# A recurrent row with its causal mask added on TensorE, and the convolution of B and C summed there from four sets of weights

## The reference

```python
def mamba2(X, W_in, conv_w, conv_b, dt_bias, A_log, D, norm_w, W_out):
    z, xBC, dt = split(X @ W_in.T)                 # 256, 384, 4 features
    dt  = softplus(dt + dt_bias)
    xBC = silu(causal_conv(xBC, conv_w) + conv_b)  # 4 taps, each of 384 channels by itself
    x, B, C = split(xBC)                           # 256 (4 heads of 64), 64, 64
    # per head: h = h * exp(dt * A) + dt * B x ;  y = C . h
    y = scan(...) + D * x
    y = y * silu(z)
    y = y * rsqrt(mean(y * y) + 1e-5) * norm_w
    return y @ W_out.T
x = layernorm(x + (mamba2(x) + x))                 # eps 1e-5
x = layernorm(x + attention_and_experts(x))        # 16 heads, 8 experts, top 2
```

## Time and profile before

| | us |
|---|---|
| runs of the kernel before: median of 3, lowest to highest | 923.86 (921.42 to 941.75) |
| profiled execution: its own time / span of the core | 919.96 / 918.3 |
| busy: TensorE | 736.6 (80%) |
| VectorE | 638.8 (70%) |
| ScalarE | 474.1 (52%) |
| GpSimd | 437.8 (48%) |
| mean granted TensorE clock | 0.914 |

### The profile page before, as it was taken

One profiled execution on the slowest core, in us unless ns is written; L12 is line 12 of the kernel. 1 busy time (PEld: TensorE's weight loads), 2 busy tenths in 40 slices (PEclk: granted clock), 3 DMA queues, 4 the chain that ended last, 5 costly groups with the idle time before them and its releaser, 6 DMA issues. The chain is left out here.

```text
span 918.3 us, 18413 instructions
## 1 busy us (share of the span) xinstructions
PE 736.6 (80%) x5462; PEld 491.5 (54%) x5462; DVE 638.8 (70%) x1576; ACT 474.1 (52%) x983; POOL 437.8 (48%) x546
## 2 busy tenths in 40 slices
PE   5978888878853979898989998989788898999500
PEld 2656555655542534444444444444347897999500
DVE  4688988898752958596868496968524576557753
ACT  3555555665420036565656455656554465666524
POOL 1344455445632112236363436363514768767863
PEclk9999999999975559999999799999979999999955
DMA  2001223432113002225252523220151222325441
GB/s 55 18 19 29 86 81 125 143 118 70 29 58 124 21 23 66 79 73 152 75 148 79 117 74 107 74 69 25 38 173 51 76 63 81 90 62 152 124 117 46
DMA packets 97998, 73.66 MB, mean 80 GB/s; under 512 B 15559, under 2 KB 89651, under 8 KB 97902
## 3 DMA queue, kind: packets, MB, share of 16 engines
q1 hardware_dynamic: 93294, 63.89, 24.6%
q0 software_dynamic: 4608, 8.60, 2.7%
HBM read 42.39 MB, written 25.25 MB: 74 GB/s over the span
## 5 line engine op out<-in xcount | busy, mean ns | idle before, releaser
L1639 ACT ACTIVATE pb<-psB 128x512 f32<-128x512 f32 (+1 forms) x352 | 192.1, 559 | 199.2 <-PE psB L2075 175.4
L1744 DVE TENSOR_REDUCE mx<-psB 128x1 f32<-128x384 f32 (+3 forms) x352 | 207.3, 634 | 64.9 <-PE psB L2055 64.6
L2053 PE MATMUL psB<-kx,qx 72*128 72x384 bf16 (+3 forms) x512 | 144.6, 333 | 17.6 <-POOL hide L1499 14.9
L2075 PE MATMUL psB<-qx,kx 75*128 75x256 bf16 (+3 forms) x512 | 131.7, 313 | 20.0 <-DMA qx<-mparts 15.5
L1596 POOL TENSOR_SCALAR_AFFINE_SELECT pb<-pb 128x512 f32<-128x512 f32 x112 | 71.0, 639 | 159.4 <-ACT pb L1639 158.5
L2055 PE MATMUL psB<-hide,ident 128*128 128x128 bf16 x512 | 109.0, 238 | 0.0
L2094 PE MATMUL psB<-pb,vx 128*32 128x512 f32 (+3 forms) x1024 | 99.4, 463 | 0.5 <-POOL pb L1596 0.5
L1565 POOL DMA_INDIRECT results<-y_e,hin x78 | 78.3, 1004 | 39.4 <-ACT y_e L1678 20.0
L2164 PE MATMUL psB<-hT_e,w1t 128*128 128x128 f32 x624 | 84.4, 278 | 14.6 <-issue 7.7
L2075 PEld LDWEIGHTS psB<-qx,kx 75*128 75x128 bf16 x512 | 46.2, 101 | 91.9 <-ACT pb L1639 55.4
L2164 PEld LDWEIGHTS psB<-hT_e,w1t 128*128 128x128 f32 x624 | 76.3, 193 | 17.4 <-issue 15.4
(11 more groups left out here) (232 smaller groups left out, 1345.0 us busy)
## 6 DMA issues: line engine op xcount, KB each, us to landing
qx<-q_parts SPq DMA_DIRECT2D x96, 96.0 KB
kx<-k_parts SPq DMA_DIRECT2D x96, 96.0 KB
hin<-slots SPq DMA_DIRECT2D x78, 65.0 KB
ys<-results SPq DMA_DIRECT2D x16, 256.0 KB, 3.9
q_parts<-part SPq DMA_DIRECT2D x8, 384.0 KB
k_parts<-part SPq DMA_DIRECT2D x8, 384.0 KB
xin<-in_L_attn_X SPq DMA_DIRECT2D x8, 256.0 KB, 3.4
x_rows<-x1o SPq DMA_DIRECT2D x8, 256.0 KB, 2.3
```

Source lines behind the costliest of these rows:

```text
L1639: nc.scalar.activation(pb[step % PBUF][:, h0:h0 + heads, 0:width], src, ACT.Exp).then_inc(exp_ready, 2 if u == NEXP - 1 else 1)
L1744: nc.vector.tensor_reduce(mx[:, h0:h0 + heads, qt], ps[:, S_BANK + u % banks, 0:heads * width].rearrange("p (h n) -> p h n", n=width), AX. ...
L2053: nc.tensor.matmul(out, qx[q][0:QK_ROWS, h0 + j, qt * P:(qt + 1) * P], kx[q][0:QK_ROWS, h0 + j, 0:width], start=True, stop=False)
L2075: ins = nc.tensor.matmul(out, kx[q][0:MAX_ROWS, 4 * g + h0 + j, kt * P:(kt + 1) * P], qx[q][0:MAX_ROWS, 4 * g + h0 + j, kt * P:SEQ], start ...
```

## The change

- **Mask.** `seg` gets a second product that adds `cover` to its bank: 0 where the causal mask keeps and -3e38 where it does not, in bf16 through a bf16 identity, so that the exponential gives 0 there. `gm` goes; each `mm` reads G straight from PSUM, bank 3. The third state product, which writes bank 3, now waits for the fourth `mm`.
- **Convolution of B and C.** At the start the block's weights are scaled by each of the four taps (`wtap`), turned on TensorE and copied (`wtapT`). `conv_bc` then sums four products of shifted inputs in bank 6, and SiLU reads that bank with the bias. The block's taps on VectorE and ScalarE are gone. The taps of x stay.
- **Residual.** `x2` goes: `woutT` is halved, the residual adds `xin` itself, and the layer norm's eps is divided by 4. `xin` gets a third buffer, which the residual of its row frees.
- **Order within a row.** On TensorE `turn_x` and `turn_xc` move to the end of a row (the first for two rows ahead, into bank 2), `project_dt` up behind `sums`. On GpSimd the second `ra_step` of a row moves behind `rms`. On ScalarE the squares of b-1 stand around the `yT` copy, half before and half behind; SiLU of B and C comes ahead of that of x.
- **End of the stage.** On VectorE the last residual moves ahead of the `rest` steps of row 6, on GpSimd `norm` and `shift` of the last row move ahead, and on SyncE the stores of row 6 move ahead of the last bf16 copy.

The core of the diff:

```diff
         def seg(pe, row, c):
             pe.wait_ge(ra_ready, row(4, c + 1))
             if c >= 2:
                 pe.wait_ge(decay_ready, row(4, c - 1))
             nc.tensor.matmul(bank(4 + c % 2), after[:, :], ra[c % 2][:, :, :].rearrange("p h n -> p (h n)"),
-                             start=True, stop=True).then_inc(seg_ps, 1)
+                             start=True, stop=False)
+            nc.tensor.matmul(bank(4 + c % 2).rearrange("p (h n) -> p h n", n=P), ident16[:, :],
+                             cover[:, :].unsqueeze(1).broadcast_to([P, MH, P]), start=False, stop=True).then_inc(seg_ps, 1)
...
+                if load:
+
+                    ahead = it * 2 + p + 2
+                    if ahead >= XBUF:
+                        sp.wait_ge(r_ready, ahead - XBUF + 1)
+                    sp.dma_start(xin[ahead % XBUF][:, :, :], x_rows[ahead]).then_inc(x_in[ahead % XBUF], 16)
...
+            store_qkv(BATCH - 2)
             store_x1b(BATCH - 1)
-            store_qkv(BATCH - 2)
...
+            nc.gpsimd.affine_select(out=ident16[:, :], in_=ones[:, :], compare_op=ALU.is_equal, fill=0.0, base=0,
+                                    pattern=[[-1, P]], channel_multiplier=1).then_inc(consts, 1)
+            nc.gpsimd.memset(cover[:, :], -3e38).then_inc(consts, 1)
+            pool.wait_ge(consts, 10)
+            nc.gpsimd.affine_select(out=cover[:, :], in_=cover[:, :], compare_op=ALU.is_gt, fill=0.0, base=0,
+                                    pattern=[[-1, P]], channel_multiplier=1).then_inc(consts, 1)
             own = Chain(pool, pool_own, 2)
...
                     rms(before)
+                ra_step(row, 1)
                 xw_step(row, 0)
...
-                pool.wait_ge(x_in[p % 2], (it + p // 2 + 1) * 16)
-                pool.wait_ge(r_ready, row(1, 0))
-                nc.gpsimd.tensor_tensor(x2[:, :, :], xin[p % 2][:, :, :], xin[p % 2][:, :, :], ALU.add).then_inc(x2_ready, 1)
                 xw_step(row, 2)
                 if it * 2 + p >= 2:
                     for n in range(2):
                         split(it * 2 + p - 2, n)
                 if not last:
-                    for c in range(2):
-                        ra_step(next_row, c)
...
             rms(Row(BATCH // 2 - 1, 1))
+            norm(Row(BATCH // 2 - 1, 1))
             for n in range(2):
                 split(BATCH - 2, n)
-            norm(Row(BATCH // 2 - 1, 1))
+            shift(BATCH - 1)
             for n in range(2):
                 split(BATCH - 1, n)
-            shift(BATCH - 1)
 
...
-                act.wait_ge(conv_done, row(3, 2))
-                if old:
-                    act.wait_ge(intra_ps, before(4, 0))
-                nc.scalar.activation(xc[q][:, :, :], acc[:, 0:2, :], ACT.Silu).then_inc(silu, 1)
-                act.wait_ge(conv_done, row(3, 3))
+                act.wait_ge(conv_ps, row(3, 3))
                 if old:
                     act.wait_ge(c_moved[q], (it + p // 2) * 16)
                     act.wait_ge(bctr_ps, before(1, 0))
                     act.wait_ge(g_ps, before(1, 0))
-                nc.scalar.activation(bc[q][:, :], acc[:, 2, :], ACT.Silu).then_inc(silu, 1)
+                nc.scalar.activation(bc[q][:, :], bank(6), ACT.Silu, bias=cb[:, 2:3]).then_inc(silu, 1)
+                act.wait_ge(conv_done, row(2, 2))
+                if old:
+                    act.wait_ge(intra_ps, before(4, 0))
+                nc.scalar.activation(xc[q][:, :, :], acc[:, :, :], ACT.Silu).then_inc(silu, 1)
...
+                    squares(before, 0)
                     yT_copy(before)
-                if not last:
-                    xT_copy(next_row)
+                    squares(before, 1)
                 cumulative(row)
...
-                    newest_tap(next_row, 2)
                     softplus_ln(next_row)
                     silus(it, p + 1)
-                squares(row)
+                if it * 2 + p + 2 < BATCH:
+                    xT_copy(it * 2 + p + 2)
             all_rows(act, body)
+            squares(Row(BATCH // 2 - 1, 1), 0)
             yT_copy(Row(BATCH // 2 - 1, 1))
+            squares(Row(BATCH // 2 - 1, 1), 1)
...
-            def masked_g(row):
-
+            def masked(row, c):
                 dve.wait_ge(g_ps, row(1, 1))
-                dve.wait_ge(m_ready, row(4, 0))
-                nc.vector.tensor_tensor(gm[:, :, :], bank(3).rearrange("p (t n) -> p t n", t=TILES),
-                                        upto[:, :].unsqueeze(1).broadcast_to([P, TILES, P]), ALU.mult).then_inc(gm_ready, 1)
-
-            def masked(row, c):
-                dve.wait_ge(gm_ready, row(1, 1))
                 dve.wait_ge(decay_ready, row(4, c + 1))
                 if row(4, c - 3) > 0:
                     dve.wait_ge(intra_ps, row(4, c - 3))
                 nc.vector.tensor_tensor(mm[c][:, :, :], decay[c % 2][:, :, :],
-                                        gm[:, c, :].unsqueeze(1).broadcast_to([P, MH, P]), ALU.mult).then_inc(m_ready, 1)
+                                        bank(3)[:, c * P:(c + 1) * P].unsqueeze(1).broadcast_to([P, MH, P]), ALU.mult).then_inc(m_ready, 1)
...
-                dve.wait_ge(x2_ready, row(1, 1))
+                dve.wait_ge(x_in[b % XBUF], 16 * (b // XBUF + 1))
...
-                                                         scalar=rstd[:, t:t + 1], in1=x2[:, t, :],
+                                                         scalar=rstd[:, t:t + 1], in1=xin[b % XBUF][:, t, :],
...
+                nc.vector.tensor_scalar(wtap[:, k, :], win[:, DI // P + 2, :], cw[:, 2, k:k + 1], None, ALU.mult).then_inc(tap_scaled, 1)
...
-            taps(start, 2)
+            dve.wait_ge(tap_ps, 1)
+            nc.vector.tensor_copy(wtapT[:, :, :].rearrange("p k n -> p (k n)"), bank(3)).then_inc(tap_sb, 1)
...
-                if not last:
-                    taps(next_row, 2)
                 y_steps(row, p)
...
+            residual(end, BATCH - 1)
             rests(BATCH - 2)
-            residual(end)
...
+            def turn_x(b):
+
+                pe.wait_ge(x_in[b % XBUF], 16 * (b // XBUF + 1))
+                if b == 1:
+                    pe.wait_ge(setup_sb, 5)
+                if b >= 2:
+                    pe.wait_ge(h_ready, 3 * (b - 1))
                 for t in range(TILES):
-                    ins = nc.tensor.transpose(bank(6)[:, t * P:(t + 1) * P], xin[p % 2][:, t, :], ident[:, :])
+                    ins = nc.tensor.transpose(bank(x_bank(b))[:, t * P:(t + 1) * P], xin[b % XBUF][:, t, :], ident[:, :])
                 ins.then_inc(xT_ps, 1)
...
-                nc.tensor.matmul(bank(6 + c % 2), winT[:, DI + c * P:DI + (c + 1) * P], xT[:, :],
+                nc.tensor.matmul(bank(6 + c), winT[:, DI + c * P:DI + (c + 1) * P], xT[:, :],
                                  start=True, stop=True).then_inc(conv_ps, 1)
+
+            def conv_bc(row):
+
+                pe.wait_ge(conv_done, row(2, 1))
+                for s in range(TAPS):
+                    ins = nc.tensor.matmul(bank(6)[:, s:SEQ], wtapT[:, TAPS - 1 - s, :], xT[:, 0:SEQ - s],
+                                           start=(s == 0), stop=(s == TAPS - 1))
+                ins.then_inc(conv_ps, 1)
...
-                pe.wait_ge(conv_done, row(3, 3))
+                pe.wait_ge(conv_done, row(2, 2))
+                pe.wait_ge(silu, row(3, 1))
...
-                pe.wait_ge(silu, row(3, 1))
-                pe.wait_ge(y_ready, row(1, 0))
+                pe.wait_ge(silu, row(3, 2))
+                pe.wait_ge(intra_read, row(1, 0))
...
-                    pe.wait_ge(gm_ready, row(1, 1))
+                    pe.wait_ge(m_ready, row(4, 4))
...
                 conv(start, c)
+            pe.wait_ge(tap_scaled, TAPS)
+            for k in range(TAPS):
+                ins = nc.tensor.transpose(bank(3)[:, k * P:(k + 1) * P], wtap[:, k, :], ident[:, :])
+            ins.then_inc(tap_ps, 1)
+            pe.wait_ge(tap_sb, 1)
+            conv_bc(start)
+            turn_x(1)
             project_z(start)
+            turn_xc(start, 0)
...
+                sums(row)
                 if not last:
-                    turn_x(it, p + 1)
-                turn_xc(row, p)
-                sums(row)
+                    project_dt(next_row)
                 if not first:
                     out_projection(before)
                 seg(pe, row, 0)
...
-                if not last:
-                    project_dt(next_row)
...
                 intra(pe, row, 0)
-                if not last:
-                    conv(next_row, 2)
                 intra(pe, row, 1)
                 state(row, 2)
                 intra(pe, row, 2)
                 intra(pe, row, 3)
+                if not last:
+                    conv_bc(next_row)
                 from_states(row, p)
+                if it * 2 + p + 2 < BATCH:
+                    turn_x(it * 2 + p + 2)
                 if not last:
                     project_z(next_row)
+                    turn_xc(next_row, p + 1)
```

100 lines of the change are left out of this document (51 added, 49 removed).

## The result

Over 20 runs each, the changed kernel takes 935.54 us (median; 924.73 to 945.55) and the kernel before 926.26 us (917.57 to 941.75). The ratios here and further down leave out every run more than 1.5% above the fastest of its kernel (here 8 of the 20 after and 6 of the 20 before; in e12 one of six, 1122.41 us at a granted clock of 0.626). The ratio is 1.008, with a 95% interval of 1.005 to 1.012. The change makes the kernel slower by some 0.8%. That lies inside the 2% that the forecast called no change, but its 919 us was on the wrong side of the kernel before, and its range, 910 to 930 us, misses the median. The profiled execution took 934.39 us, its span 932.7.

A forecast was written before the change was run, and what follows sets the result against it. VectorE set the old pace; TensorE's taps now join the chain. Steady rows 0.4 us longer, second row's `y` 5.8 later, last row 6.0 later, end 7.55 earlier: next stage 1.6 earlier, 919 us, range 910 to 930.

The forecast's parts named there:

- The steady row: Recurrent stage, one batch row: the chain from rates to rates sums to 31.2 us against 30.82, 0.4 us longer.
- the group: TensorE's four B/C tap products, ahead of the states' products: 4 x 0.86 plus 0.09 us, 3.53 us a row.
- a cover: The mask's added bf16 product in each of four `seg` steps: 0.31 us, between 0.22 and 0.43.
- the multiply: VectorE's fourth mask multiply, now reading G from PSUM: priced at 0.66 us instead of 1.67, with 1.67 as other bound.
- VectorE stays the bound: Rival: the four taps fit TensorE's slack, so a row takes 28.5 us and the kernel 898 us; chance 0.09.
- the odd columns cost: Rival: tap products writing from columns 1 to 3 take double, 18 us in seven rows, 937 us; chance 0.06.
- The first rows: Start of the recurrent stage: `y` of row 0 at 55.2 us, of the second row at 84.7, 5.8 us later.
- a start at either clock level: Allowance in the forecast's own range for the start's products running at 2.4 or 1.2 GHz: -4 or +3 us.
- The last row and the end: Last row 24.8 us, its `y` 6.0 us later; from there to the next stage 7.55 us less.
- the edits at the end don't act: Rival: the next stage waits for transfers to land, so 4.95 us are not gained, 924 us; chance 0.13.
- The sum of the stage: Whole recurrent stage: 6.0 us later at the last `y` less 7.55 at the end, next stage at 292.4 us.
- the signs that the forecast named: Profile checks: period 30.9 to 31.6 us, taps 3.4 to 3.6, cover 0.2 to 0.4, stage 290 to 295 us.

The follow-up runs named there:

- e12: Changed kernel, B/C taps back on VectorE, last shifted copy before row 6's splits, two unread products per row in TensorE's waits; 905.75 us, 0.978 of the kernel before.
- e3: Changed kernel with only the newest of the four B/C tap products kept; rows 2, 3 and 6 take 28.34 us, against 30.9.
- e6: Kernel before with only the mask's part (second product in `seg`, no `gm`, later third state product); a row of 30.81 us.
- e9: Changed kernel with one and two unread fp32 products ahead of the third state product in rows 0 and 1; row 1 29.22 us, next stage at 293.56.
- e5: Kernel before with only the new order at the stage's end; 27.2 us from the last `y` to the next stage, where it was 34.4.
- e11: Kernel before with the new end, plus the last shifted copy and its store ahead of row 6's splits and theirs; 918.93 us against 923.40, ratio 0.993.
- e10: Changed kernel, B/C taps back on VectorE, one unread product per row in TensorE's wait for `y`, last shifted copy before row 6's splits; 910.54 us, ratio 0.985.

## Why the prediction was wrong

- **The steady row: right.** Forecast 31.2 us, measured 30.9; VectorE's wait before `t1` 3.5 and 3.36, the group 3.53 and 3.48, a cover 0.31 and 0.22, the multiply 0.66 and 0.68. e3 shows that the group is paid one for one. The rivals "VectorE stays the bound" and "the odd columns cost" fall with the same rows. What stood ahead of it, that VectorE ran nearly without a gap and alone set the pace before, was wrong in part (its 2.5 us of waits, e6); the layout did not use it.
- **The first rows: the step that failed** is a clock term put at nothing. The forecast put `y` of row 0 at 55.2 us, of row 1 at 84.7, and the steady rows at 31.2 from there. Measured, with the start of the transposes less 0.26: 57.35, 91.58, and row 2 at 32.56. The misses are 2.1, 4.7 and 1.4 us; the first holds 3.4 us of the clock and a `dt` projection that came 0.8 us early (30.06 and not 30.9). The forecast allowed for "a start at either clock level" alone; it took every later group at the upper level, as in the rows that it read. Several ran at the lower one, which cost 10.2 us beyond the steady durations in three rows, and since the change had moved TensorE onto the path, nearly all of it was paid. The kernel before has such stretches too, and the forecast passed over them. Its TensorE timeline:

```profile
105.50 3.68 PE L906 MATMUL psA<-winT,xT 128*128 128x256 f32 x8 [1.53 <-DVE acc L667]
109.75 1.09 PE L966 MATMUL psA<-ident,y 128*128 128x128 f32 x8 [0.57 <-DVE y L769]
```

  The `z` projection at 105.50 takes 1.7 us more than at 198.34, and the wait ahead of the transposes of `y` shrinks from 2.25 to 0.57: the row stays at 30.82, and only the next one is 0.4 us longer. There VectorE's work hid the stretch. e9 shows that without the stretches row 1 takes 29.2 us, against the 29.5 of the sum: the mechanism of the row was right, and a term for the clock was missing. It is 8.2 us by the three misses; e9 took back 6.5.
- **The last row and the end: right, nearly.** 24.4 us and not 24.8. The end gave back 6.7 us and not 7.55; on the kernel before the same edits gave 7.2 (e5), where the last output projection took 2.05 us and not 2.96. The stall of `x1o`, 2.5 us by e11, was not foreseen, and without it the end would have been better than forecast: that the sum came close is in part luck. The rival "the edits at the end don't act" falls.
- **The sum of the stage**: forecast 1.6 us earlier, measured 6.1 later. The misses 2.1 + 4.7 + 1.4 in the first rows, -1.2 in rows 3 to 6, -0.4 in the last row and +0.9 at the end make 7.5 of the 7.7 us between 292.4 and 300.09. The forecast of no change at 2% came true all the same, since that band is 18 us wide. Of the signs that the forecast named, only the stage's length failed (300.09 us and not 290 to 295).
- **The level: a second step that failed.** The prediction was put at 919 by the profiled execution, 919.96 us, with the remark that the median shown was 3.9 us higher, and the range was centred there. The median of 20 runs is 926.26, and one execution is a poor base where 20 of the same kernel lie between 917.57 and 941.75 us. 926.26 less 1.6 would have been 924.7; with the 7.7 us missed in the stage, 932.4, and 935.54 was measured. The other 3.1 us are not traced; they are less than the rest differs from trace to trace.

What stays open is what makes the clock fall. Filling a wait removed the stretch behind it in e9 and e12, so the wait has a part in it, but a wait is not enough by itself:

- e10 has the same waits, 0.52 and 0.54 us, ahead of the projections of rows 1 to 7, and rows 1, 2 and 7 keep the upper level (2.03 to 2.05 us). The changed kernel and e3 have 0.26 and 0.54 us in nearly all rows, and some fall.
- Rows 3 to 6 of the kernel before wait 1.53 and 2.25 us, and their products stay at the upper level; row 2 has the same 1.53 us, and its `z` projection (105.50) falls.
- In e9 the output projection behind row 0's `y` lost its stretch too (2.03 us, and 2.93 in the changed kernel), with the 0.26 and 0.54 us ahead of it unfilled.
- In e10 the projection shrinks from row to row (3.46, 3.32, 3.17, 3.04 us) with the waits unchanged.
- The product that fills a wait also puts a full-sized product between transposes and small sums. No run separates this from the idle time, and none varied the length of one wait by itself.

## What to carry to other kernels

An engine that comes off the slack and onto the path brings its clock with it: read how often its rows in the trace run at the lower level under cover of another engine, and price every new product on the path at both levels. When a price is the same work at two durations, look at what the engine did just before; here short waits came ahead of the slow stretches, though not every such wait had one behind it, and in e12 a product that nobody reads, put into such a wait, was worth more than it cost (1.6 us a row for 0.86 us of work). And price the parts of a change apart: the reordered end was worth 7 us by itself, and the convolution on TensorE hid it.

## What the runs showed of the hardware

- Behind waits of 0.52 and 0.54 us TensorE ran an output projection partly at 1.2 GHz (e10, row 6), and wholly at 2.4 GHz when the second of them was filled (e12): 3.04 against 2.03 us for the same 16 instructions. The same two waits in e10's row 2, and 2.25 us in the kernel before, had no such stretch behind them.
- A VectorE step with two operands in SBUF took 3.70 us beside GpSimd's casts and subtractions, and 1.14 without them (e5, e11).
- Products that write from columns 1, 2 and 3 of a bank cost what those from column 0 cost: 3.48 us for four, 0.87 each.
